# The last two sequence chunks of a fused four-layer kernel: a new order on all engines, all deltas on TensorE, and bn_aggr for the moments

## The reference

```python
def step(S, kvq):                                  # S: (rows, 32 blocks, 8, 8)
    k_t, v_t, q_t = kvq
    k_norm = k_t / (jnp.linalg.norm(k_t, axis=-1, keepdims=True) + 1e-06)
    retrieved = jnp.einsum('bnij,bnj->bni', S, k_norm)
    delta = v_t - retrieved
    S_new = jnp.tanh(S + jnp.einsum('bni,bnj->bnij', delta, k_norm))
    Sq = jnp.einsum('bnij,bnj->bni', S_new, q_t).reshape(B_, n)
    return (S_new, Sq * jax.nn.silu(Sq))           # scanned over the 4 batch rows; 1024 positions side by side
x = _layernorm(x + _L1_attn_ref(x, ...))
xr = mu_r * x + (1.0 - mu_r) * x_prev              # x_prev: x one position earlier
xk = mu_k * x + (1.0 - mu_k) * x_prev
r = jax.nn.sigmoid(jnp.einsum('btc,dc->btd', xr, W_r))
k_act = jnp.square(jax.nn.relu(jnp.einsum('btc,dc->btd', xk, W_k)))
x = _layernorm(x + r * jnp.einsum('btc,dc->btd', k_act, W_v))
```

## Time and profile before

| | |
|---|---|
| median of 3 runs | 1132.73 us |
| the profiled execution's own time | 1132.0 us |
| its span in the trace | 1130.1 us |
| TensorE busy / weight loads | 1097.6 us (97%) / 855.1 us (76%) |
| VectorE busy | 944.7 us (84%) |
| ScalarE busy | 592.3 us (52%) |
| GpSimd busy | 512.2 us (45%) |
| first instruction of VectorE for chunk 7's x2 in `finish()` | at 1044.44 us |
| last compute instruction | from 1125.99 us, 0.41 us |

### The profile page before, as it was taken

One profiled execution on the slowest core, in us unless ns is written; L12 is line 12 of the kernel. 1 busy time (PEld: TensorE's weight loads), 2 busy tenths in 40 slices (PEclk: granted clock), 3 DMA queues, 4 the chain that ended last, 5 costly groups with the idle time before them and its releaser, 6 DMA issues.

```text
span 1130.1 us, 16851 instructions
## 1 busy us (share of the span) xinstructions
PE 1097.6 (97%) x5925; PEld 855.1 (76%) x5925; DVE 944.7 (84%) x1415; ACT 592.3 (52%) x988; POOL 512.2 (45%) x426
## 2 busy tenths in 40 slices
PE   9999999999999999999999999999999999999786
PEld 4566666678787777878778877878787788778575
DVE  4788888973034998999899889989998998899898
ACT  2345555555435355645655574556456555754544
POOL 1466677676333244324433432443244334364653
PEclk9999999999999999999999999999999999999899
DMA  7346555623531440423132323404231323231001
GB/s 262 109 158 246 205 202 201 247 100 112 168 112 49 139 130 19 130 80 127 56 113 83 123 74 111 148 19 124 81 128 51 116 78 108 75 112 57 1 1 40
DMA packets 45131, 127.03 MB, mean 112 GB/s; under 512 B 4368, under 2 KB 21520, under 8 KB 43152
## 3 DMA queue, kind: packets, MB, share of 16 engines
q1 hardware_dynamic: 43920, 114.20, 30.3%
q10 hardware_dynamic: 1152, 12.07, 2.9%
HBM read 117.86 MB, written 19.92 MB: 122 GB/s over the span
## 4 chain that ended last, share of the span: by engine, by line
PE 73%; DVE 16%; POOL 4%; issue 3%; ACT 2%; DMA 0%; SPq 0%; POOLq 0%; DVEq 0%; ACTq 0%
PE lower L1243 43%; PE bank L1243 17%; PE lower L440 5%; PE lower L572 2%; POOL state L748 2%; POOL rgn L757 2%; PE bank L1232 1%; DVE tmp L2290 1%; DVE tmp L2276 1%; PE bank L487 1%; DVE Sq L2278 1%; DVE tmp L2301 1%; DVE y L847 1%; DVE delta L2297 1%; DVE S L2303 1%
## 5 line engine op out<-in xcount | busy, mean ns | idle before, releaser
L2059 POOL TENSOR_TENSOR a_lo<-whole,a_hi 128x512 fp32r<-128x512 f32 x128 | 181.6, 1435 | 260.3 <-ACT a_hi L1644 172.4
L1243 PE MATMUL lower<-b_hi,ring 128*128 128x512 f32 x512 | 193.8, 396 | 1.4 <-ACT a_hi L1644 1.4
L1243 PE MATMUL lower<-b_lo,ring 128*128 128x512 f32 x512 | 190.9, 391 | 1.7 <-POOL b_lo L2059 1.7
L1243 PE MATMUL lower<-a_hi,ring 128*128 128x512 f32 x496 | 187.5, 394 | 0.0
L1243 PE MATMUL lower<-a_lo,ring 128*128 128x512 f32 x496 | 185.4, 390 | 0.0
L2059 POOL TENSOR_TENSOR b_lo<-whole,b_hi 128x512 fp32r<-128x512 f32 x64 | 93.5, 1469 | 144.4 <-ACT b_hi L1644 125.8
L1627 ACT ACTIVATE S<-S 128x1024 f32<-128x1024 f32 x56 | 58.6, 1059 | 172.8 <-DVE S L2303 168.9
L1643 ACT ACTIVATE whole<-lower,hs 128x512 f32<-128x512 f32 x126 | 86.2, 685 | 81.0 <-PE lower L1243 79.2
L1243 PEld LDWEIGHTS lower<-b_hi,ring 128*128 128x128 f32 x512 | 96.2, 188 | 21.9 <-issue 1.8
L1243 PEld LDWEIGHTS lower<-b_lo,ring 128*128 128x128 f32 x512 | 96.1, 188 | 21.9 <-POOL b_lo L2059 2.3
L440 PE MATMUL lower<-wa,xT 128*128 128x512 f32 x240 | 109.3, 599 | 2.1 <-DVE turned L817 1.4
(11 more groups left out here) (293 smaller groups left out, 2418.8 us busy)
## 6 DMA issues: line engine op xcount, KB each, us to landing
ring<-ffn_copy_dram SPq DMA_DIRECT2D x128, 512.0 KB, 3.5
look<-ffn_dram ACTq DMA_DIRECT2D x6, 1879.0 KB, 6.9
ffn_copy_dram<-ffn_dram SPq DMA_DIRECT2D x4, 2112.0 KB, 9.7
rope<-rope_dram SPq DMA_DIRECT2D x8, 512.0 KB, 8.0
xtok<-x_dram SPq DMA_DIRECT2D x8, 512.0 KB, 4.1
x1in<-x_dram SPq DMA_DIRECT2D x8, 512.0 KB, 4.8
x1res<-x_dram SPq DMA_DIRECT2D x8, 512.0 KB, 3.1
xT<-xT_dram SPq DMA_DIRECT2D x7, 512.0 KB, 8.3
```

The costliest lines, as they stand in the source:

```text
L1243: ins = nc.tensor.matmul(out, a, b, start=(first and n == 0), stop=(last and n == len(pairs) - 1))
L2059: nc.gpsimd.tensor_tensor(lo[:, m, :], t["whole"][:, m % 4, :], hi[:, m, :].bitcast(F32), ALU.subtract).then_inc(lo_done, 1)
```

## The change

All edits lie in `finish()`, apart from the helpers for moments and the shape of `times`. Beside the order of nearly all calls:

- row 0's delta is formed by TensorE too, and `times` is written in the state's own order, so that TensorE reads it with a step of 8 values instead of in one piece;
- the seven small operations of `row_moments` become one bn_aggr for each row and one or two small operations;
- the key norms are made for rows 0-1 together and rows 2-3 together (before: 0, 1, 2-3), and x2's moments for row 0, row 1, rows 2-3 (before: 0, 1-3);
- `left_keys(0)` is cut in two, with row 0's deltas between, and `left_gates(1)` likewise;
- chunk 6's `earlier_read(1)` stands between the rows of chunk 7's x2;
- GpSimd's `read_q` waits for both halves of `times_key`, no more for its own only.

```diff
-            BY_TENSOR = (1, 2)
+            BY_TENSOR = (0, 1, 2)
...
+            for n, b in enumerate(range(rows.start, rows.stop)):
+                ins = nc.vector.bn_aggr(out=mv[:, b, :], in_=st[:, n, :])
+            steps.done(ins)
             steps.wait()
...
+            if negated:
+                nc.vector.tensor_scalar(mv[:, rows, 0], mv[:, rows, 0], -1.0, None, ALU.mult)
+            nc.vector.tensor_scalar(mv[:, rows, 1], mv[:, rows, 1], EPS, None, ALU.add).then_inc(ve_ready, 1)
...
-                        product(tensor_delta(hf), [(ident[:], x) for x in (v, *(t["times"][:, hf, j, :] for j in range(BS)))]
+                        product(tensor_delta(hf).rearrange("p (n i) -> p n i", i=BS),
+                                [(ident[:], x) for x in (v.rearrange("p (n i) -> p n i", i=BS),
+                                                         *(t["times"][:, hf, :, :, j] for j in range(BS)))]
...
                     turn_left(0)
-                    left_keys(0)
+                    left_keys(0, range(0, 1))
+                    delta(0, 0)
+                    delta(0, 1)
+                    left_keys(0, range(1, KD))
...
-                            pool.wait_ge(fin_times_k, step_of(s, hf))
+                            pool.wait_ge(fin_times_k, step_of(s, 1))
...
-                    key_root(0, slice(0, 1))
-                    key_root(1, slice(1, 2))
+                    key_root(0, slice(0, 2))
```

**ScalarE, start.** Of the reordered calls, these are the ones on which chunk 6's gate and the first states hang: 

```diff
-                    query_row(0)
-                    x2_row(1)
-                    x2_row(2)
-                    turned_row(1)
-                    earlier_silu()
-                    x2_row(3)
+                    earlier_square()
                     key_square(1)
                     key_value_row(0)
...
+                    state_tanh(0, 0)
+                    query_row(3)
+                    left_normed(0)
                     state_tanh(0, 1)
```

More of the change, by code:

```diff
@@ L141, in build, with row_stats @@
         pow_ready = sem(top, "pow_ready")
-        def row_stats(steps, r, rows):
-            for b in rows:
-                ins = nc.vector.bn_stats(out=stats[:, b, :], in_=r[:, b, :])
+        def row_stats(steps, r, rows, st=None):
+            for n, b in enumerate(rows):
+                ins = nc.vector.bn_stats(out=stats[:, b, :] if st is None else st[:, n, :], in_=r[:, b, :])
             steps.done(ins)
@@ L1509, in left_keys @@
                             pe.wait_ge(left_relu, min(g, 3))
-                        for m in range(KD):
+                        for m in part:
                             ins = product(keys[:, m * width:m * width + width].rearrange("p (b n) -> p b n", n=P),
@@ L1524, in left_gates @@
                             pe.wait_ge(left_sig, min(g, 3))
-                        for r, b in enumerate(range(*LEFT[g][1:])):
+                        for b in part:
+                            r = b - LEFT[g][1]
                             ins = product(gates[:, r * DIM:r * DIM + DIM],
@@ L1560, in finish @@
                     left_keys(1)
-                    left_gates(1)
+                    left_gates(1, range(2, 3))
                     delta(2, 0)
+                    delta(2, 1)
+                    left_gates(1, range(3, BATCH))
                     left_values(1)
                     turn_left(2)
-                    delta(2, 1)
                     left_keys(2)
@@ L1977, in finish @@
                     mix_gates(4)
-                    for g in ENDS[:-1]:
+                    for g in ENDS[1:-1]:
                         result_rows(g)
@@ L2486, in earlier_moments @@
                     def earlier_moments():
-                        moments(ln3, x3, t["mv3"], ve3)
-                        ln3.end()
+                        st = end_stats[:, 2 * BATCH:3 * BATCH]
+                        ln3.wait()
+                        row_stats(ln3, x3, range(BATCH), st)
+                        row_moments(ln3, t["mv3"], slice(0, BATCH), ve3, st)
                     def ffn_row(b):
@@ L2525, in keys_scaled @@
                     def keys_scaled(b):
-                        after("keys", min(b, 2))
+                        after("keys", b // 2)
                     def first_state(hf):
-                        k, v, _, _, _, w = last_parts(0, hf)
+                        k, v, _, _, w = last_parts(0, hf)
                         dve.wait_ge(fin_turned, BATCH)
@@ L2613, in x3_moments @@
                         after("x3", g)
-                        row_stats(fin, x3, range(rows.start, rows.stop))
-                        row_moments(fin, t["mv3"], rows, ve3)
+                        st = end_stats[:, BATCH + rows.start:BATCH + rows.stop]
+                        row_stats(fin, x3, range(rows.start, rows.stop), st)
+                        row_moments(fin, t["mv3"], rows, ve3, st, g < FINAL)
                     def normed_by_hand(g, r, mv, rstd, rooted, count):
```

191 lines of the change are left out of this document (90 added, 101 removed).

## The result

The changed kernel takes 1141.55 us (median of four runs, 1141.08 to 1143.11), and the kernel before, on the same chip, 1132.70 us. The ratio is 1.0076, with an interval of 1.0064 to 1.0089: 8.8 us slower, where 1.1 us faster was forecast. The profiled execution took 1141.18 us with a span of 1139.4 us (before: 1132.0 and 1130.1).

A forecast was written before the change was run, and what follows sets the result against it. VectorE was taken to bound the last 90 us, except TensorE at the end; some 10 us of relief mostly became waits. Last turning 0.7 and moments 0.4 us earlier gave -1.1 us: 1131.6 against the median, range 1128.8 to 1139.5.

The forecast's parts named there:

- rival 1: TensorE's deltas: reading `times` 8 values apart adds up to 1.95 us each, +7.2 us in all, 1139.9; chance 0.27.
- a delta is 2.0 us: Row 0's deltas on TensorE: each takes 2.0 us as before, so `outer` (0,0) starts at 1072.8.
- the clock: TensorE at group 0's half keys: a drop to 1.2 GHz behind idle time ends them at 1070.65 rather than 1069.6.
- group 2's keys: TensorE's keys near the end: start at about 1103.6 us against 1102.48 before, 1.1 us later.
- `outer` (0,0): Row 0's first outer product on VectorE: starts at 1072.8 against 1072.76 before, after a wait of some 3.3 us.
- gate, and its wait: Chunk 6's gate on VectorE: reached at about 1053.2, 3.9 us earlier, its 2.80 us wait gone.
- one hit on GpSimd's root: GpSimd's root for rows 0-1: one small operation slowed by VectorE, 1.14 us instead of 0.29, +0.85.
- wait for the key norms: VectorE, done with chunk 6's moments by 1058.7, waits 2.6 us for the roots, ready at 1061.3.
- first state: After the key norms and 1.4 us of scaling: starts at 1062.7 against 1061.22 before, 1.5 us later.
- from there to the last turning: TensorE from group 2's keys on: 13.3 us in one piece against 15.1 before, last turning at 1116.9, 0.7 us earlier.
- Rival 2: The waits laid in for TensorE's clock and GpSimd's root don't come: 1129.7, or 1128.7 without delta (1,0)'s wait; chance 0.30.
- rival 3: Clock drops also in the keys of rows 2 and 3 and behind new idle: +2.3 us, 1135.0; chance 0.05.

The follow-up runs named there:

- e1: The changed kernel with the layout of `times` from before put back (TensorE reads in one piece, VectorE writes with a step): 1138.54 us.
- e2: The kernel before with the new layout of `times` alone, row 0's delta still on VectorE: 1136.3 us.
- e15: The changed kernel, step of 8 values kept, with five useless TensorE products of 256 columns ahead of group 0's turning: 1139.78 us.
- e3: The changed kernel with `times` in pairs: TensorE reads two neighbouring values then steps, VectorE writes two operations of 512 values: 1136.84 us.
- e9: The changed kernel with `times` in pairs and five useless TensorE products ahead of group 0's turning only: 1134.51 us.
- e5: The changed kernel with `times` in pairs and useless TensorE products in two idle stretches, five before group 0's turning, eleven before group 2's: 1131.74 us.
- e12: The changed kernel with pairs and both fillers, VectorE's mixing of group 0 put ahead of row 1's two sums: 1131.73 us.
- e7: The kernel before with bn_aggr alone in its ten sets of moments, order and layout as they were: 1130.53 us.

## Why the prediction was wrong

**The step that failed** is the choice between the forecast and rival 1 in the costing of TensorE's read: "a delta is 2.0 us", with the step of 8 values held for free. I gave the rival 0.27 because 0.95 ns is more than a cycle; no row showed a read with such a step. A record of 128 columns now takes 3.89 / 16 = 0.24 us, 1.9 ns a column. e1 and e2 show that the step does it, e15 its price: 8.0 us, within about 2, where rival 1 had worked out 8.3. This near a meeting is partly luck, with such a margin. The Trainium skill's rule ("Advanced Engine Details and Errata", SBUF Cachelines) was the right guide: two hits on a 16-byte line were wanted, the step of 8 values gives one, and e3's pairs, which give two, run at 1.95 us. The traces agree on both sides.

**The second term, mis-sized**, is the clock. The mechanism was right and its place too: a drop at group 0's half keys, behind TensorE's idle time. It cost them 1.6 us (3.60 instead of the 1.99 of e15) and not 1.05, and at the end 1.8 us (the changed kernel less e15's 1139.74) to 2.3 (e3 less e9). The forecast's own working slips here besides: turned rows at 1068.1 and 1.75 us of keys make 1069.85, not 1069.6. Before the change a drop lay there too, but VectorE did row 0's deltas itself and had no wait for TensorE between 1062 and 1112 us. Putting the deltas behind the half keys took this cover away. A second drop, at group 2's keys, is missing in the changed kernel's profile. It is in the profiles of e1, e3 and e9, where the deltas are quick and TensorE idles 4.8 to 5.4 us for the norms of group 2, so making the deltas cheap alone gives 4.7 and not 8 us. But e15's profile has it with slow deltas and 1.10 us of idle time, so a long idle stretch is not the whole condition, and what is stays open.

**What closes the sum.** The forecast 1131.6, the step's 8.0, and 0.8 more for the clock (1.8 at the end instead of 1.05) make 1140.4. The last 1.2 us is what e5 stands above the forecast without its clock term (1131.74 - 1130.55). As each term is the difference of two of these times, the sum closes by itself and proves none of them. Most like it is VectorE's mixing of group 0, held up by GpSimd's read (2.36 us from 1101.15). The first line below is from before, the second from the changed kernel:

```profile
1090.52 0.68 DVE L2637 SCALAR_TENSOR_TENSOR y<-y,x 128x512 f32<-128x512 f32 x1
```

```profile
1102.02 2.04 DVE L2634 SCALAR_TENSOR_TENSOR y<-y,x 128x512 f32<-128x512 f32 x1
```

I had priced GpSimd's delay by VectorE and never the other way round. That this 1.36 us is the remainder is argued, not shown: e12 moved it and could not take it away.

**What held, and where it broke.** Up to the products the forecast held within 0.5 us; the two rows that did not hold are `outer` (0,0) and group 2's keys.

| step | forecast | measured |
|---|---|---|
| gate, and its wait | 1053.2 us, none | 1053.61 us, 0.41 us |
| one hit on GpSimd's root | +0.85 us | first operation 1.20 us instead of 0.29 |
| wait for the key norms | 2.6 us | 2.55 us |
| first state | 1062.7 us | 1063.20 us |
| products of row 0 | 1065.1, 1067.3 us | 1065.52, 1067.68 us |
| bn_aggr | near 0.16 us | 0.18 us, some 0.07 more for each further row |
| `outer` (0,0) | 1072.8 us | 1075.85 us |
| group 2's keys | 1103.6 us | 1113.96 us |
| from there to the last turning | 13.3 us | 13.34 us |

The first outer product is 3.05 us late: 0.9 by the half keys, 1.9 by the delta's step, the rest in small terms. The new order itself is worth little, and e5 and e7 show why: bn_aggr alone gives 1.85 us in the old order, and the new order with bn_aggr, pairs and full clock gives 0.6. Its 3.5 us of lead at the gate are spent on the wait for norms made in one piece and on deltas that stand behind the keys. Rival 2 (the waits don't come) is refuted. Of rival 3 only the further drop behind a new idle stretch came, in the experiments; the drop in the keys of rows 2 and 3 is in no profile of the new order.

## What to carry to other kernels

When a layout is changed for the engine that writes, price the read on the other engine by a row with the same step, or take a layout that keeps two neighbours together: here the pairs gave both engines nearly their full rate. An engine taken off the critical path by one edit may idle, lose its clock and give the gain back on its next work, so walk the idle stretches of TensorE in the new order and ask what stands directly behind each. And an operation is free only for its own engine: row 0's deltas cost TensorE 4 us of work and took the cover from a stretch at the low clock for which VectorE had not waited before.

## What the runs showed of the hardware

- TensorE with 4-byte values, read 8 values apart: 3.89 us for 16 records of 128 columns, against 1.95 in one piece, in runs of 8, or in pairs 16 values apart.
- VectorE, 1024 products of 4-byte values: 1.21 us in one piece, 1.92 written with a step of 128 values, 1.97 read with a step of 8, and 1.29 as two operations written with a step of 2.
- GpSimd's reads of 2.36 us hold up some VectorE operations that meet them: one of 512 values on two SBUF operands took 2.04 us instead of 0.68, a tensor_scalar of 64 integers 1.91 instead of 0.20 (changed kernel, 1102.02 and 1069.54 us), while an outer product that reads PSUM ran beside GpSimd at its 1.22 us (e5, 1096.09 us). The Trainium skill ("SBUF — State Buffer", SBUF: two separate sides) tells of a port pair that one of the two engines holds for a whole instruction; the traces agree.
- TensorE's granted clock was 0.50 (1.2 GHz) for 6 us behind idle stretches of 2.43 and 4.79 us (e3). Behind 1.10 and 0.68 us it was 0.50 for some 3 us in e15's profile and stayed at 1.00 in the changed kernel's. By their mean clock, 0.999 in three and 0.997 in two, executions of e15 on one chip differed in it.
